# Attention scores of a Trainium2 kernel on column tiles of four heads, and half of the convolution's scores placed ahead of a wait

## The reference

```python
query, key_ = relu(f[:, :, :d]), relu(f[:, :, d:2 * d])
value_pad = concat([value, ones])                        # 9 rows
scores = einsum('bhdn,bhen->bhde', value_pad, key_)      # 9x8 a head
out = einsum('bhde,bhen->bhdn', scores, query)
out = out[:, :, :-1] / (out[:, :, -1:] + EPS)
```

## Time and profile before

| | us |
|---|---|
| median of three runs | 4757.51 (4748.52 to 4766.44) |
| the profiled execution's own time | 4761.0 |
| its span, first to last instruction | 4759.2 |
| PE busy | 4475.4 (94%) |
| PE weight loads busy | 3665.0 (77%) |
| DVE busy | 2811.9 (59%) |
| ACT busy | 2208.0 (46%) |
| POOL busy | 1239.6 (26%) |

### The profile page before, as it was taken

How to read it: one execution, slowest core, us unless ns; L and a number is a source line. 1 busy time by engine, 2 the same in 40 slices (tenths; PEclk the granted TensorE clock), 3 DMA queues, 4 the chain that set the end, 5 groups by cost and what they waited for, 6 DMA issues and landing times. The chain is left out here.

```text
span 4759.2 us, 70417 instructions
## 1 busy us (share of the span) xinstructions
PE 4475.4 (94%) x24296; PEld 3665.0 (77%) x24296; DVE 2811.9 (59%) x4023; ACT 2208.0 (46%) x3983; POOL 1239.6 (26%) x1030
## 2 busy tenths in 40 slices
PE   8999999999999999999999999589999999999968
PEld 7988988888888889888888888466666676666626
DVE  3354454454444444543544444279889978978996
ACT  3343333343333433433333334046576666666666
POOL 2442433433424424324334244000030020003003
PEclk9999999999999999999999999799999999999989
DMA  6685676676766766856767667767557746746613
GB/s 192 223 286 198 232 270 211 230 256 223 255 221 236 272 201 231 286 200 225 259 223 254 226 229 246 259 221 243 174 181 224 244 142 221 247 161 201 201 56 126
DMA packets 486662, 1045.54 MB, mean 220 GB/s; under 512 B 40624, under 2 KB 94512, under 8 KB 484016
## 3 DMA queue, kind: packets, MB, share of 16 engines
q1 hardware_dynamic: 486320, 1040.99, 65.1%
HBM read 665.02 MB, written 375.82 MB: 219 GB/s over the span
## 5 line engine op out<-in xcount | busy, mean ns | idle before, releaser
L807 POOL TENSOR_TENSOR toeplitz<-taps 128x512 f32<-128x512 f32 x768 | 895.7, 1193 | 932.3 <-PE bank L483 864.2
L483 PEld LDWEIGHTS bank<-toeplitz,columns 128*128 128x128 f32 x8192 | 964.3, 193 | 15.3
L483 PE MATMUL bank<-toeplitz,columns 128*128 128x128 f32 x8192 | 963.7, 276 | 0.0
L391 PE MATMUL bank<-x_hi,w_hi 128*128 128x512 f32 x1536 | 612.0, 398 | 19.8 <-DVE x_lo L655 19.8
L393 PE MATMUL bank<-x_lo,w_hi 128*128 128x512 f32 x1536 | 601.0, 391 | 0.0
L392 PE MATMUL bank<-x_hi,w_lo 128*128 128x512 f32 x1536 | 599.1, 390 | 0.0
L1530 POOL TENSOR_TENSOR centred<-centred,x_out 128x512 f32<-128x512 f32 x128 | 174.3, 1384 | 1606.8 <-ACT centred L1313 1605.1
L742 DVE TENSOR_SCALAR ckey_t<-bank 128x256 f32<-128x256 f32 x256 | 108.5, 424 | 807.5 <-PE bank L483 807.5
L473 PE MATMUL bank<-loaded,toeplitz 128*128 128x256 f32 x2048 | 510.9, 394 | 57.7 <-DMA loaded<-tiles_dram 42.1
L1163 PE MATMUL bank<-edge,w_branch 128*128 128x512 f32 x1024 | 483.2, 621 | 78.6 <-ACT edge L1261 78.6
L1149 PE MATMUL bank<-att_hi,w_proj_hi 128*128 128x512 f32 x1024 | 437.5, 427 | 62.3 <-DMA att_lo<-att_dram 51.2
(11 more groups left out here) (142 smaller groups left out, 7036.7 us busy)
## 6 DMA issues: line engine op xcount, KB each, us to landing
x_sb<-in_x_tiled SPq DMA_DIRECT2D x128, 1024.0 KB, 6.3
loaded<-tiles_dram SPq DMA_DIRECT2D x256, 433.5 KB, 5.9
tiles_dram<-tiles SPq DMA_DIRECT2D x112, 867.0 KB, 7.6
inverse<-inverse_dram SPq DMA_DIRECT2D x256, 256.0 KB, 7.7
att_dram<-out_hi SPq DMA_DIRECT2D x256, 256.0 KB, 4.1
att_dram<-out_lo SPq DMA_DIRECT2D x256, 256.0 KB, 5.1
att_hi<-att_dram SPq DMA_DIRECT2D x64, 1024.0 KB, 7.6
att_lo<-att_dram SPq DMA_DIRECT2D x64, 1024.0 KB, 10.5
```

Source lines behind the costliest of these rows:

```text
L391: nc.tensor.matmul(banks[t][:, :], wh, xh, start=(k == 0), stop=False)
L483: last = nc.tensor.matmul(bank[:, v * M:(v + 1) * M], columns[:, h % 2, t - T_K, v + b, a * HT:(a + TO) * HT], w[:, t, d, :], start=(d == ...
L807: last = nc.gpsimd.tensor_tensor(toeplitz[:, h % 2, t, :].rearrange("p (d o r) -> p d o r", o=HD, r=PL), tap, point, ALU.mult)
```

## The change

The 128 channels of an iteration are 4 quads of 4 heads (32 channels). A score matmul of 128 weight columns and 129 moving columns becomes four, one a quad, with 32 weight columns and 33 moving ones (32 values and ones), each at its own column tile of the array and on its own 32 partitions of `SCORE_BANK`. The layouts of `value_t` and `cvalue_t` get a column of ones for each quad. In the conv stage the scores are taken in two halves, first quads 0 and 1 over all 32 blocks, which need heads 0 to 7 only, then quads 2 and 3, which wait for all 16 heads; the wait for the last copy of q comes after both. DVE masks the four quads' diagonal blocks by four instructions; the rest of `score_n` stays zero from one memset at the start.

```diff
+        QUADS = 4
+        QD = P // QUADS
+        QH = QD // HD
-        value_t = sb("value_t", [P, 2, 4, P + 1])
+        value_t = sb("value_t", [P, 2, 4 * QUADS, QD + 1])
-        cvalue_t = sb("cvalue_t", [P, HV * PL, P + 1])
+        cvalue_t = sb("cvalue_t", [P, HV * PL, QUADS, QD + 1])
...
                     for n in range(4):
-                        last = nc.tensor.matmul(SCORE_BANK[:, 0:P + 1], key_t[:, j % 2, n, :], value_t[:, j % 2, n, :],
-                                                start=(j == 0 and n == 0), stop=(j == NCH - 1 and n == 3))
+                        for i in range(QUADS):
+                            last = nc.tensor.matmul(SCORE_BANK[i * QD:(i + 1) * QD, 0:QD + 1], key_t[:, j % 2, n, i * QD:(i + 1) * QD],
+                                                    value_t[:, j % 2, QUADS * n + i, :],
+                                                    start=(j == 0 and n == 0), stop=(j == NCH - 1 and n == 3), tile_position=(0, i * QD))
...
+                def conv_score(it, half):
+                    heads = SH * (it + 1) - (SH // 2 if half == 0 else 0)
+                    pe.wait_ge(cevac[T_K], heads)
+                    pe.wait_ge(cevac[T_V], heads)
+                    for n in range(HV * PL):
+                        for i in range(QUADS // 2 * half, QUADS // 2 * (half + 1)):
+                            last = nc.tensor.matmul(SCORE_BANK[i * QD:(i + 1) * QD, 0:QD + 1], ckey_t[:, n, i * QD:(i + 1) * QD],
+                                                    cvalue_t[:, n, i, :],
+                                                    start=(n == 0), stop=(n == HV * PL - 1), tile_position=(0, i * QD))
+                    if half:
+                        last.then_inc(scores_ready, 1)
...
-                    for t in range(3):
-                        pe.wait_ge(cevac[t], SH * (it + 1))
                     pe.wait_ge(w_out_ready, START + 2 * it + 1)
-                    for n in range(HV * PL):
-                        last = nc.tensor.matmul(SCORE_BANK[:, 0:P + 1], ckey_t[:, n, :], cvalue_t[:, n, :],
-                                                start=(n == 0), stop=(n == HV * PL - 1))
-                    last.then_inc(scores_ready, 1)
+                    conv_score(it, 0)
+                    conv_score(it, 1)
+                    pe.wait_ge(cevac[T_Q], SH * (it + 1))
...
-                    copy(value_t[:, j % 2, :, 0:P], VALUE_BANK[:, :].rearrange("p (n m) -> p n m", m=P)).then_inc(value_t_ready, 1)
+                    copy(value_t[:, j % 2, :, 0:QD], VALUE_BANK[:, :].rearrange("p (n m) -> p n m", m=QD)).then_inc(value_t_ready, 1)
...
-                        to = cvalue_t[:, :, h * HD:(h + 1) * HD].rearrange("p (s r) o -> p s r o", s=HV)
+                        to = cvalue_t[:, :, h // QH, h % QH * HD:(h % QH + 1) * HD].rearrange("p (s r) o -> p s r o", s=HV)
...
-                    nc.vector.tensor_copy(key_sum[:, :], SCORE_BANK[:, P:P + 1]).then_inc(key_sum_ready, 1)
+                    nc.vector.tensor_copy(key_sum[:, :], SCORE_BANK[:, QD:QD + 1]).then_inc(key_sum_ready, 1)
...
-                    nc.vector.tensor_tensor(score_n[:, :].rearrange("p (h d) -> p h d", d=HD),
-                                            SCORE_BANK[:, 0:P].rearrange("p (h d) -> p h d", d=HD),
-                                            mask[:, :, None].to_broadcast([P, SH, HD]), ALU.mult).then_inc(scores_masked, 1)
+                    for i in range(QUADS):
+                        of = slice(i * QD, (i + 1) * QD)
+                        last = nc.vector.tensor_tensor(score_n[of, of].rearrange("p (h d) -> p h d", d=HD),
+                                                       SCORE_BANK[of, 0:QD].rearrange("p (h d) -> p h d", d=HD),
+                                                       mask[of, i * QH:(i + 1) * QH, None].to_broadcast([QD, QH, HD]), ALU.mult)
+                    last.then_inc(scores_masked, 1)
...
+                    nc.vector.memset(score_n[:, :], 0.0)
```

More of the change, by code:

```diff
@@ L767, in first @@
                     nc.vector.tensor_tensor(scale_row[:, :], scale_row[:, :], out_sb[:, 0, :], ALU.mult).then_inc(bn_inverted, 1)
-                    nc.vector.memset(value_t[:, :, :, P:P + 1], 1.0)
-                    nc.vector.memset(cvalue_t[:, :, P:P + 1], 1.0).then_inc(cleared, 1)
+                    nc.vector.memset(value_t[:, :, :, QD:QD + 1], 1.0)
+                    nc.vector.memset(cvalue_t[:, :, :, QD:QD + 1], 1.0).then_inc(cleared, 1)
                     dve.wait_ge(cleared, 3)
```

## The result

| | before | after |
|---|---|---|
| median of six runs, us | 4758.83 (4748.52 to 4766.93) | 4730.75 (4717.0 to 4734.63) |
| profiled span, us | 4759.2 | 4727.8 |
| ratio of the times | | 0.9937, 95% interval 0.9919 to 0.9955 |

The change saves 28 us where 81 were forecast: the right sign, but about a third of the size. It missed the forecast's own range, 4652 to 4700; the wider one, 4650 to 4752, held only because it reached to a rival that did not come true. The profiled spans differ by 31.4 us.

A forecast was written before the change was run, and what follows sets the result against it. PE time was taken as kernel time in the changed stages, except at named waits. Sum: 15 x (1.9 + 3.67) + 1.9 + 1.9 - 6 = 81 us, so 4757.5 - 81 = 4677 us; own range 4652 to 4700, wider 4650 to 4752.

The forecast's parts named there:

- a rival that did not come true: Floor that all tiles share, for chunk and conv scores: just under the deciding point, no gain, 4750 us; chance 0.13.
- The cost of tiled records: Score matmuls: four places give a 128-position block in 0.064 us instead of 0.225; turns 0.23; chunk scores 0.49 instead of 0.89.
- Both rival floors: Minimum time per score record: near 0.026 us no gain, 4750 us, chance 0.13; at 0.055 us slower, 4965 us, chance 0.11.
- The order rule: Matmuls start and end strictly in program order: a chunk's scores cost 0.51 us instead of 0.26, time about 4692 us.
- The plain stage: Scores of chunks 0 to 5 save 2.4 us, less 0.5 of new waiting for `x_lo` at chunk 6: 1.9 us an iteration.
- the step for the clock: Start of a conv stage, after the thin stretch: more half clock, charged 0.4 us an iteration, 6 in all.
- The last scores and `denominate` "gain nothing": End of the plain stage: the wait for the first head's tiles, hanging on the last `qkv`, covers the 0.6 us saved.
- The conv stage: Last k and v matmuls to next `qkv`: 4.17 us instead of 7.84, so 3.67 us saved an iteration.
- The rival that came true: Conv scores: fetching 512 instructions takes 5.9 us against 4.1 of work, giving 4706 us; chance 0.14.
- Another sign: Sign that the forecast is wrong: gaps inside the conv scores that start with an instruction fetch.
- The last iteration: Last conv scores to `denominate`: limited by the convolved queries, ready at 2987.5, it can gain 1.9 us only.
- Masking: DVE after the scores: four instructions instead of one of 283 ns cost under 1 us, needed much later; effect nothing.

The follow-up runs named there:

- e4: The change, with the first half of the conv scores (quads 0 and 1) moved from behind head 15 to behind head 11; 4663.91 us.
- e1: The change with its conv scores, their layout and mask taken back, so only the plain stage's scores are on column tiles; 4699.37 us.
- e5: The change with conv scores on two column tiles of 64 columns instead of four of 32, 256 instructions in one burst after all waits; 4643.4 us.
- e10: e4 with only 16 of the first half's 32 blocks behind head 11, the rest at the end, 384 instructions in a row; 4645.04 us.
- e2: The change with its plain scores taken back, so only the conv stage's scores are on column tiles; 4779.45 us.
- e6: The kernel before, with two iterations in the loop's body so that half the jumps go; 4712.41 us.
- e3: The change, with conv scores after all copies, the four quads of a block one behind the other at four places; 4737.61 us.
- e9: e4 with only 24 of the first half's 32 blocks behind head 11, the rest at the end; 4658.23 us.

## Why the prediction was right or wrong

**The cost of tiled records: right.** A chunk's scores save 0.36 us where 0.40 was forecast, both turns included, and a half of the conv scores takes 2.16 us for the forecast 2.05 (e4). Both rival floors, 0.026 us a record and above, are out: the 32 records of a chunk start within 0.39 us, 12 ns each. The order rule is out as well: by it the 32 records alone were to take 0.51 us, without the turns. Reading the overlap off `denominate` was sound.

**The plain stage: near by itself, in part by luck, and 0.8 us short in the change.** 1.9 was forecast as 2.4 less a new wait of 0.5 for `x_lo`. e1 has 2.1, which is six times 0.36; the wait did not come (19.2 us for 19.8 in the change, 16.7 in e1). The change has 1.1, since the step for the clock looked at the wrong place. It charged 0.4 us for the start of the conv stage; the dip came at the start of the plain stage, behind the standstill. In those places the change stands at half clock for 54.6 us and the kernel before for none. After the first such stage, those with a dip take 78.75 us in the mean and the two without one 77.65. At the starts of the conv stages the time at half clock became less instead, 47.8 us for 75.1.

**The last scores and `denominate` "gain nothing": wrong, by 1.3 us an iteration.** "That transfer hangs on the last `qkv`" was true, but the transfer did not always end the wait. The row that spoke against it was in the same view: PE's wait at L473 has a second entry, not among the rows shown, 12.4 us of "issue" in 3 waits:

```profile
PE bank L473 <- issue: 12.4, 3, 4.2
```

I took the name at the end of a wait for its cause, and the landing for something that the scores cannot move. In 8 of 13 iterations of the kernel before PE waited beyond the landing, and the landing itself came 0.7 us sooner after its issue when `denominate` came 0.6 us sooner (4.00 for 4.69). So the wait for `loaded` did not grow by 0.6 to 1 us, as forecast: with "issue" it went from 54.5 us in all to 45.2.

**The conv stage: this is the step that failed.** "The first half has no wait left and starts on the heels of the last convolution" held. "2798.48 to the next `qkv` becomes 4.17 us instead of 7.84" did not: it took 8.51. The term that failed is 4.17: it had 2 x 2.05 us of arithmetic and nothing for bringing in 512 instructions. 3.67 us an iteration were expected, and 0.67 lost.

**The rival that came true was there, with too low a price.** "Instructions come too slowly" was worked out at 5.9 us for the burst, from the landing time of a small transfer, and given 0.14. The fetches in the burst are 3.5 us apart, not 2.6, and the first comes only after some 4 us. With 8.51 for the end, and the clock that follows it, the books give: forecast 81, less (8.51 - 4.17) x 15 = 65 for the burst, less 0.8 x 15 = 12 in the plain stage, plus 1.3 x 15 = 20 in the thin stretch, plus 6 for the charge that was put at the conv start: 30 us, against 31.4 between the spans (the heads' 0.2 us an iteration and the last iteration's loss are left out, and nearly cancel). The price of the rival left out that the clock falls behind a standstill, though a clock at 0.5 in the first `qkv` stood among the signs. Another sign was off: the gap does not start with a fetch, but 1.1 us ahead of it.

**The last iteration** gained 0.2 us at its end and not 1.9: the end of the last convolution to `denominate` was 8.60 us (2980.79 to 2989.39), now 8.39 (2949.61 to 2958.00), with the same standstill in it.

**Masking: right.** Four instructions of 185 ns for one of 283, off the path:

```profile
L665 DVE TENSOR_TENSOR score_n<-bank,mask 32x32 f32<-32x32 f32 x128 | 23.7, 185 | 1.3
```

## What to carry to other kernels

Spread such a burst between longer instructions, or take the coarser tile that halves the count, even if its arithmetic doubles: here pairs of 64 columns in one burst (e5, 4643.4) and quads of 32 with a part of them moved between the heads (e10, 4645.04) came out level, some 87 us under quads of 32 in one burst. At the end of a loop body, look at what the jump stands behind; a "DMA" or "issue" wait right after it may be the fetch of the next instructions or a load that runs beside it, and work just before it on another engine may be worth more than its own length. Ask when the data landed (another engine that reads the same tile tells) before you believe either name.

## What the runs showed of the hardware

- Instructions arrive in blocks of 256: each fetch is 16.4 KB, and 12288 more records bring 48 more fetches (e5: 8192 and 32). Records are not all that counts: e1 and e2, with 6144 more each, have 16 and 29 more fetches, and e6, with the same records and half the jumps, 16 fewer. In a burst they start 3.5 us apart, and PE stands still some 540 instructions after the start of the last fetch before the burst; the change, e3, e4, e5 and e9 fit, and e10 in all but its first and last iteration. That PE holds exactly two blocks is the simplest reading of these counts, not something a record shows; nor does any show when a fetch is asked for, only when its transfer starts.
- Behind standstills of 3.4 to 4.1 us the clock was at 0.50 around the start of 13 of 15 plain stages, for 3.4 to 6.8 us, which cost the stage about 1 us (78.65 for 77.68).
- Column tiles overlap in f32 even where each matmul is two records: 32 records of 33 columns at four places take 0.39 us from start to start, and both turns some 0.14 more (0.09 into the tiles, 0.06 back); at two places 128 records take 2.16. The Trainium skill (TensorEngine Tiling, Instruction Overhead) puts some 60 cycles on a matmul, 25 ns at 2.4 GHz; the 12 ns a record here are less than half, though the two records of an f32 matmul together take as long.
- The loop's jump ahead of the first head costs time: 7.7 to 8.6 us from the last `qkv` without it, in the kernel before 9.1 to 10.9 with it and in the change 8.5 to 9.2. The delay of what stands before the jump is not passed on one for one (0.61 became 1.1). In the kernel before, the first head starts at 9.1 to 9.3 where the fetch starts 1.2 or 1.3 us after `denominate` does (in one of these five iterations at 10.6, with a fetch of 2.76 us), and at 10.3 to 10.9 in the eight where it starts 2.4 to 3.4 us after. What sets off the fetch sooner or later stays open.
- A load of the first head's tiles lands 3.0 to 3.4 us after its issue in the three iterations of the kernel before without a fetch beside it, and 3.0 to 5.9 in the 13 with one.
